# Who issues the transfers that bring an attention output to its rows: from SP's queue to ACT's

## The reference

```python
h1 = ln(x);  x = attn(h1, h1, wq, wk, wv, wo, ...) + x      # self-attention, 16 heads of 16, fake-quantised to 8 bits
h2 = ln(x);  x = attn(h2, context, ...) + x                  # cross-attention to 77 keys, quantised
h3 = ln(x);  x = a * gelu(g) @ ff_w2 + x                     # a, g = split(h3 @ ff_w1)
# second layer
x = x + cross_attn(rmsnorm(x), rmsnorm(context)) @ Wo        # 16 query heads, 4 key heads of 64, rotary positions
x = x + (silu(y @ Wgate) * (y @ Wup)) @ Wdown                # y = rmsnorm(x)
```

## Time and profile before

| | |
|---|---|
| device time, median of 3 runs | 2571.34 us (2564.44 to 2571.38) |
| device time of the profiled execution | 2566.87 us |
| span of its profile | 2565.1 us |
| granted TensorE clock over the span | 0.876 |
| busy: PE / DVE / ACT / POOL | 1997.6 / 1810.0 / 1136.4 / 935.8 us |
| one full step | 142 to 146 us |

### The profile page before, as it was taken

How to read it: one execution, slowest core, us unless ns; L and a number is a source line. 1 busy time by engine, 2 the same in 40 slices (tenths; PEclk the granted TensorE clock), 3 DMA queues, 4 the chain that set the end, 5 groups by cost and what they waited for, 6 DMA issues and landing times.

```text
span 2565.1 us, 41654 instructions
## 1 busy us (share of the span) xinstructions
PE 1997.6 (78%) x10552; PEld 1431.5 (56%) x10552; DVE 1810.0 (71%) x3327; ACT 1136.4 (44%) x1906; POOL 935.8 (36%) x1629
## 2 busy tenths in 40 slices
PE   3665587878887887878888887879787887878786
PEld 3323265656665565656665565646565565656665
DVE  1566777696878777696877778686878778685632
ACT  1244535545454545545454545545353445444211
POOL 1213334343434334343434334343434334343212
PEclk8666698989999898989998898989888898989888
DMA  7486453634445353634445363634435353635010
GB/s 233 103 162 132 82 122 62 134 62 98 100 80 122 74 129 61 134 62 99 99 80 122 70 133 61 135 59 98 93 76 116 71 121 63 130 55 106 1 35 5
DMA packets 761579, 242.61 MB, mean 95 GB/s; under 512 B 675643, under 2 KB 757295, under 8 KB 761199
## 3 DMA queue, kind: packets, MB, share of 16 engines
q1 hardware_dynamic: 758127, 241.34, 45.0%
q10 hardware_dynamic: 3328, 0.01, 0.1%
HBM read 83.57 MB, written 19.25 MB: 40 GB/s over the span
## 4 chain that ended last, share of the span: by engine, by line
PE 46%; DVE 20%; issue 15%; ACT 7%; DMA 4%; SPq 4%; POOL 3%; DVEq 1%; ACTq 0%; POOLq 0%
PE work L1394 21%; PE work L1404 16%; ACT E L899 3%; PE rowps L1465 3%; DVE scaled_row L1055 3%; DVE Pn L1062 3%; DMA PT<-Pn 3%; PE outps L1450 2%; DVE hids L1202 2%; POOL scs L797 1%; DVE st L1078 1%; ACT hTs L875 1%; PE work L1387 1%; DVE xs L1192 1%; DVE scs L1216 1%
## 5 line engine op out<-in xcount | busy, mean ns | idle before, releaser
L1055 DVE TENSOR_SCALAR_CACHE_REDUCE scaled_row<-rowps,der 128x1024 uint8<-128x1024 f32 x512 | 654.8, 1279 | 359.1 <-PE rowps L1465 358.8
L899 ACT ACTIVATE E<-rowps,ebias,der 128x1024 f32<-128x1024 f32 x512 | 614.8, 1202 | 404.4 <-DVE scaled_row L1055 310.5
L1062 DVE TENSOR_SCALAR Pn<-E,rowinv 128x1024 int16<-128x1024 f32 x512 | 395.4, 772 | 113.0 <-DMA PT<-Pn 76.6
L731 POOL TENSOR_TENSOR rowden<-rowsum,raw 128x1 f32<-128x1 f32 x512 | 118.3, 231 | 948.7 <-ACT E L899 947.4
L1465 PE MATMUL rowps<-KC,QP 16*128 16x512 bf16 x1024 | 220.7, 428 | 212.4 <-ACT E L899 200.6
L734 POOL TENSOR_TENSOR rowinv<-rowden,minus 128x1 f32<-128x1 f32 x512 | 323.4, 632 | 91.4 <-POOL rowden L731 91.4
L1394 PE MATMUL work<-hTs,ff_w_sb 128*128 128x256 f32 x1024 | 259.5, 408 | 13.0 <-ACT hTs L875 13.0
L1465 PEld LDWEIGHTS rowps<-KC,QP 16*128 16x128 bf16 x1024 | 49.0, 92 | 379.9 <-ACT E L899 247.4
L1394 PEld LDWEIGHTS work<-hTs,ff_w_sb 128*128 128x128 f32 x1024 | 201.6, 203 | 59.0 <-issue 16.0
L1559 PE MATMUL work<-K,hids 128*128 128x154 f32 x1024 | 153.5, 301 | 35.0 <-DVE scs L1216 21.4
L1559 PEld LDWEIGHTS work<-K,hids 128*128 128x128 f32 x1024 | 137.2, 190 | 53.7 <-DVE scs L1216 27.8
(11 more groups left out here) (143 smaller groups left out, 3269.7 us busy)
## 6 DMA issues: line engine op xcount, KB each, us to landing
VW<-vw_dram SPq DMA_DIRECT2D x32, 640.0 KB, 4.8
KC<-k_dram SPq DMA_DIRECT2D x128, 64.0 KB, 2.3
VB<-v_dram SPq DMA_DIRECT2D x64, 128.0 KB, 3.1
PT<-Pn SPq DMA_TRANSPOSE x512, 3.1
V<-v_dram SPq DMA_DIRECT2D x16, 320.0 KB, 3.6
vw_dram<-scs SPq DMA_DIRECT2D x32, 154.0 KB
K<-k_dram SPq DMA_DIRECT2D x16, 308.0 KB, 3.3
K<-k_dram SPq DMA_DIRECT2D x32, 154.0 KB, 3.2
```

What stands on the lines that cost most here:

```text
L731: nc.gpsimd.tensor_tensor(rowden[:, n:n + 1], rowsum[:, n:n + 1], raw[:, DW1:DW1 + 1], ALU.mult).then_inc(row_den.sem, 1)
L899: nc.scalar.activation(E[:, slot, :], rowps[n % 2][:], ACT.Exp, bias=ebias[:, n:n + 1], scale=der[:, AL1:AL1 + 1], accum_out=rowsum[:, n:n ...
L1055: nc.vector.tensor_scalar(scaled_row[:, n % 2, :], rowps[n % 2][:], der[:, NAL1:NAL1 + 1], 3.0e38, ALU.mult, ALU.min, accum_out=ebias[:, n ...
L1062: nc.vector.tensor_scalar(Pn[:, n % 2, :], E[:, ring(n)[0], :], rowinv[:, n:n + 1], 255.0, ALU.mult, ALU.min).then_inc(row_round.sem, 1)
```

## The change

ACT issues the four transfers itself, right behind its scaling, and SP no longer does. Before it issues, ACT waits for `o_ready`, that is for its own scaling to be written, and at quad 0 for `l_filled`, that is until the previous unit's `wo` has read `oT` (the same two waits that SP had). `o_out`, which `wo` and ACT's next scaling wait for, is incremented as before, and PE waits for `o_ready` as before.

```diff
@@ attn_sync @@
-            def output(quad):
-                o_ready.wait(sp, v, quad + 1)
-                if quad == 0:
-                    l_filled.wait(sp, v - 1, 1)
-                for j in range(4):
-                    h = (4 * quad + j) % H
-                    sp.dma_start(oT[DH * (h % 8):DH * (h % 8) + DH, h // 8, :], OS[32 * j:32 * j + DH, :]
-                                 ).then_inc(o_out[j].sem, 16)
...
-                quad = (n - LAG - 9) // 8
-                if (n - LAG - 9) % 8 == 0 and (parts["old"] if quad < 0 else parts["attn"]):
-                    output(quad)
@@ attn_act, output(quad) @@
                 nc.scalar.activation(OS[:], outps[:, 0:CH], ACT.Copy, scale=der[:, OSC1:OSC1 + 1]).then_inc(o_ready.sem, 1)
+                o_ready.wait(act, v, quad + 1)
+                if quad == 0:
+                    l_filled.wait(act, v - 1, 1)
+                for j in range(4):
+                    h = (4 * quad + j) % H
+                    act.dma_start(oT[DH * (h % 8):DH * (h % 8) + DH, h // 8, :], OS[32 * j:32 * j + DH, :]
+                                  ).then_inc(o_out[j].sem, 16)
```

## The result

The changed kernel takes 2616.78 us (median of 4 runs, 2607.95 to 2625.56), the kernel before, run beside it, 2567.89 us (2560.46 to 2571.38): 1.0187 times as long, 95% interval 1.0155 to 1.0218; the medians are 49 us apart. The profiled execution took 2625.56 us (span 2623.8 us) and lies at the upper end of its four; against the profiled one of before it is 58.7 us longer, and that is the difference that the traces must account for. The mean granted clock of TensorE fell from 0.876 to 0.857.

What follows compares the result with a forecast made beforehand. No engine was taken as full; PE was busy 78%, DVE 71%. Hold 18.6 + last steps 1 + clock 10 - SP 5.5 = +24 us on 2566.87 us gave 2591, or 2595 us as median; range 2562 to 2618 us.

Steps and rivals of the forecast that it cites:

- ACT's burst: Behind ACT's scaling, four issues plus a wait and lost overlap start its next instruction 2.7 us later; ends 1.8 and 3.4.
- PE's pause: PE's idle time before `wq` at quad 3 grows from 0.70 us to 3.4 us.
- The vanished wait of `wo` for oT: At quad 3 PE's 0.97 us wait for `oT` vanishes inside PE's delay; no gain counted.
- Quads 0 to 2: ACT's next exponential is late but has room; nothing counted at a 2.7 us hold, 6.5 us at 3.4 us.
- Steps 12 to 15: Quad 3 there: DVE is late by itself and absorbs most of the delay; 1 us in all.
- The hold at quad 3: In steps 2 to 11 `hTs` holds PE's `wq`, making row tile 8 late: 18.6 us in all.
- the room of 1.05 us: At quad 3 in eight of ten steps, DVE does not notice the first 1.05 us of PE's delay.
- The clock: After PE's 3.4 us pause before `wq` the clock falls to half: 10 us over ten steps, ends 0 and 20.
- SP's relief: Two bursts off SP's queue in the set-up step and the one after save 5.5 us; full steps gain nothing.
- SP's wait for POOL: In full steps SP stands behind stores waiting for POOL's `qkb`, 36.9 us, so losing its bursts buys nothing.

Runs made afterwards that it cites:

- e3: Changed kernel with ACT's four issues moved behind the other layers' activations of the same turn, at quad 3 behind `hTs`: 2570.86 us.
- e8: Kernel before with only quad 3's transfers issued by ACT, behind `hTs`; quads 0 to 2 on SP: 2581.77 us.
- e2: Changed kernel with only quad 3's transfers on ACT, right behind the scaling; quads 0 to 2 back on SP: 2615.6 us.
- e1: Changed kernel with quad 3's four transfers back on SP; quads 0 to 2 stay on ACT: 2580.87 us.
- e4: Changed kernel with six extra small products on PE in the pause before `wq`, which overwrites their result: 2589.13 us.
- e9: Kernel before, transfers on SP, with fourteen small activations on ACT behind the scaling of each quad 3: 2582.52 us.
- e5: Kernel before with two of quad 3's four transfers issued by ACT and two by SP; quads 0 to 2 on SP: 2594.35 us.
- e12: Kernel before with quads 0 to 2 issued by ACT behind the other layers' activations; quad 3 on SP: 2587.73 us.
- e10: Kernel before with fourteen small activations on ACT behind quad 3's scaling and six extra products on PE before `wq`: 2581.4 us.
- e11: Kernel before with seven small activations on ACT behind the scaling of each quad 3, transfers on SP: 2605.29 us.

## Why the prediction was right in direction and too small in size

**Right as it stood.** ACT's burst: 2.7 us said; `hTs` at +2.61 us instead of -0.12 us, 2.73 us. PE's pause: 3.4 us said, 3.42 us measured. The vanished wait of `wo` for oT: gone, and worth nothing, as said; in e3 and e8 the pause behind it is no longer cut in two and has a fall of the clock behind it. Quads 0 to 2: nothing on top of quad 3 that the medians tell (e2 2615.6 us, the changed kernel 2616.78 us), though by themselves they cost 14 us in e1. The traces do show 3.4 us, once, in the step behind the set-up: quad 3 of step 2 ends its scaling at 363.3 us in the changed kernel and at 359.9 us in e2, where those quads are SP's (e1 has it at 368.5 us, but e3 at 359.1 us, with those quads ACT's in both). Steps 12 to 15, in the sum with +1 us, came out 1.7 us shorter.

**The hold at quad 3: 18.6 us, right.** The step was "8 x (2.7 - 1.05) + 2 x 2.7", a mean of 1.86 us by which row tile 8 is late. e4, where the clock is kept up, measures it: row 8 at 7.60 us instead of 5.70 us in all ten, 1.90 us. Ten times that is 19 us. e9, held 0.89 us, less than the room of 1.05 us, has row 8 in time (5.89 us) in seven of ten steps and at 7.42 us in the three where the clock fell.

**The clock: 10 us, mis-sized.** This is the term that failed, and it failed twice over. At quad 3 the row is late by 3.81 us in the changed kernel and by 1.90 us in e4: 1.91 us a step, 19 us. The prediction reasoned that some falls would meet evacuations that DVE comes to late anyway; none did, row 8 is 9.0 us or more behind `OS` in all ten, and the upper end given, 20 us, was the value to take. The other part was not in the sum at all. Behind row 8 a step still grows by 2.2 us (the column "rest"), though nothing there waits for ACT. There lie 6.0 of the 10.9 us of additional half clock. What half clock costs away from a pause can be read inside the kernel before: 146.1 us against 141.9 us for steps with 30.7 and 17.1 us of it, 0.31 us of time for each us. (The short step also has row 8 at 4.87 us in place of 5.92 us; two steps with row 8 alike, 146.0 us with 30.7 us and 143.1 us with 20.5 us, give 0.29.) 6.0 us at 0.31 are 1.9 us a step. Only 0.7 us of them are seen directly, in the two stretches between row tiles 14 and 16 and 26 and 28, long in five of the nine steps instead of three; the rest is this estimate. A step is then longer by 1.9 (hold) + 1.9 (clock behind the pause) + 1.9 (clock elsewhere) = 5.7 us, and nine by 51 of the 53.7 us that the trace has; the 3.4 us of quads 0 to 2 and small differences of both signs make up the 58.7. The medians are only 49 us apart, since the profiled run of the changed kernel lies 9 us above its median.

By the same two terms (row 8, and 0.31 us for each us of half clock beyond the first 12 us behind `OS`) e2 should be 5.4 us a step longer (measured 5.2), e9 1.7 (1.8), e5 2.5 (3.0), e1 1.4 (2.0), e12 1.2 (1.6), e4 2.4 (2.1), e10 1.7 (2.2), e3 -0.2 (0.4). It fails for e11, 2.5 us against 4.4, and for e8, 0.7 against 2.2. So the price of 0.31 us is an estimate and not a law.

**SP's relief: 5.5 us, did not come.** Quad 3 of unit 0 ends its scaling at 232.7 us, against 232.3 us before. In e3, where the transfers are ACT's as well but stand behind its other work, it ends at 229.5 us. So 2.8 us are to be had there, and the hold on ACT takes them back, which the prediction had granted for one burst of the three only. Even in e3 they are mostly lost again one step later (359.1 us at quad 3 of step 2, against 359.5 us).

**SP's wait for POOL** is 43.3 us instead of 36.9 us, and DVE's for the transposes 64.8 us (54 times) instead of 76.6 us; DVE's waits for transposes are thus 11.8 us less, but its waits for `rowps` are 396.3 us in place of 358.8 us, and it is no sooner for it.

**What is open.** Why the clock falls at a given place in one step and not in the same place of the next, and so why a kernel goes to and fro or settles. What a fall costs in such a stretch is shown (1.5 to 1.7 us from row tile 26 to 28, in every case), and with it most of what e1 and e12 lose with row 8 on time. That the rest of the remainder is the clock's too is argued from the 0.31 us, which leaves 0.4 to 0.6 us a step unexplained in e1 and e12 and more in e8 and e11. Whether four transfers on ACT cost more than an equal hold without them was not measured, since e9's hold came out at a third of theirs. e4 and e10, both filled, are 22 and 14 us slower than the kernel before run beside them; row 8 is 0.9 us later in e4 in each of ten steps, which accounts for the difference and leaves little for the transfers themselves.

## What to carry to other kernels

A DMA issued by ACT was an instruction of 0.6 us on that engine: ask what stands behind it in that queue, and put it behind the activation that another engine waits for (2616.78 us against 2570.86 us here, for a move by a few instructions). Where TensorE's clock is in play, a pause has three prices: its own length less the room, the slow matmuls right behind it, and the slower course that the following steps may fall into; take the last from steps of different length in the trace of before. An edit near such a loop may cost 0.6 to 0.7% with the row that was feared for on time (e1, e8, e12), so that a gain of that size must be shown by timing and not by a vanished wait; none of the twelve variants was faster than the kernel before.

## What the runs showed of the hardware that was not expected

- TensorE doing twelve matmuls more behind each quad 3 made the changed kernel 27.7 us faster (e4), as the clock stayed up through `wq`, 3.72 us in all ten steps.
- Identical code with an identical pause of 1.22 us ran `wq` at 3.72 us and at 5.41 us in one execution (e11), and its steps went from 146 to 150.2 us and stayed there. The length of the pause in front of a stretch doesn't by itself say which level it gets; what the clock was some microseconds ahead of `OS`, at 1.00 in the one and at 0.50 in the other, goes with it. In e5, e9 and e11 together, with pauses of 1.22 to 2.39 us, a fall followed the pause in 14 of 17 steps with half clock in the 12 to 5 us before the end of `OS`, and in none of 13 without.
- The same stretch of the loop, row tile 26 to 28, took 6.0 us without half clock and 7.5 to 7.7 us with 3.4 us of it, in 126 steps of fourteen traces without an exception.
- Four issues on ACT take 2.46 us, 0.61 us apiece, the same as on SP (2.45 us), and ACT does nothing else meanwhile. The 50 ns for dispatching a DMA in the Trainium skill (DMA: Bandwidth & Descriptors, "Anatomy of one DMA — SWDGE (gpsimd) path") are for GpSimd's path, and no run here shows that path; for ACT's they would be too little by a factor of twelve.
- Activations of 16 columns follow one another every 0.08 us (fourteen in 1.15 us), where one of 256 columns takes 0.47 us.
